# Third attention's lead in another order on three engines, and the wait for its last stores moved past a block boundary

## The chip, the core and the metric

The kernel runs on one core of one Trainium2 chip. The metric is the device time of one launch in microseconds (us), the median of several runs. The core has a matrix engine (PE), a vector engine (DVE), a scalar engine (ACT), a general-purpose engine (POOL) and a sequencer that only issues transfers here (SP). Each runs its own list of instructions in order; between them there are only semaphores.

## The reference

Two layers of a hybrid network over 1024 tokens of width 256, in float32. Layer 0 runs twice "attention, then a mixture of 64 experts" (block-causal attention, then windowed attention). Layer 1 runs "full attention, feed-forward, latent attention, feed-forward". What matters here is the first part of layer 1, the third attention of the kernel:

```python
Xn = (X - mu) * rsqrt(var + 1e-5) * ln_w + ln_b          # X is itself a layer norm of the stream
Q, K, V = split(Xn @ W_in)                                # 16 heads of 16, over 4 x 256 tokens
Q, K = rope(Q), rope(K)                                   # interleaved pairs, first 8 channels of a head
probs = softmax(Q @ K.T / sqrt(16))                       # nothing is masked
out = (probs @ V) @ W_out + X
```

In this launch x is (1, 1024, 256), so that each query sees all 1024 keys.

## The kernel before

The program is two blocks, one behind the other. Class First (its engines' lists are First.sync, .tensor, .scalar, .gpsimd and .vector) holds both layers of experts with the attentions before them (tags a and b), and then the **lead** of the third attention (tag c). Class Second begins with the third attention itself. Between the two stands Core.clear_semaphores: at the end of a block every engine waits for the others, then GpSimd clears First's semaphores, in ranges, and all engines meet once more. Semaphores made with keep=True are left out of the clearing; they keep their counts into Second. So nothing of Second starts before the slowest engine of First has come to its end.

**What the lead computes.** The projection Q, K of tile t (128 tokens) goes to PSUM (Projection.project, `project(t)`), ACT copies it out (`copy(t)`), and DVE (even tiles) or POOL (odd tiles) rotates it (`rotate`: two products into a side buffer, a product and a sum in place). For exact products in bfloat16 each value is then held as a sum of three bfloat16 parts. That is done in eight units n, each a chunk of 128 rows for one half of the tokens:

- `turn(n)` on PE: four transposes into PSUM bank 4 or 5. Waits for the rotations of its half, and for rest(n-2), which frees the bank.
- `part1(n)` on ACT: PSUM to the first part.
- `rest(n)` on DVE: PSUM minus the first part, into one of three buffers.
- `part2(n)` on ACT: rest to the second part.
- `part3(n)` on POOL for even n, on DVE for odd n: rest minus the second part.
- `store(n)` on SP: the three parts to DRAM, 384 KB. In Second, SP issues 78 transfers that read them back, stacked by head (Projection.stack).

The first stacks are not read back but made on the chip: `make(n)` on PE, n = 0 to 11, is three matmuls that pick rows out of the three parts of a unit (unit 0 for n = 0 to 3, unit 1 for 4 to 7, unit 4 for 8 to 11), into PSUM bank 6 or 7; `mcopy(n)` copies the result out, on ACT for even n and on DVE for odd n, and frees the bank for make(n+2).

**The order before.** PE: turn 0, 1, 2, 3 between and behind the last projections; make 0 to 3; turn 4; make 4 to 7; turn 5, 6, 7; make 8 to 11. ACT, DVE and POOL have their own lists written out by hand to match (First.scalar, First.vector, First.gpsimd). At the end of First.sync stands

```python
for n in range(1, 2 * c.per_half):
    c.store(sp, n)
sp.wait_ge(c.parts_stored, 16 * 2 * c.per_half)
```

and in Second.sync `c.stack(sp, h, g, 0)`, whose 0 says that no wait is wanted.

**Ahead of the lead.** The norm of the second half of the tokens is turned by PE into banks 6 and 7 (`norm.turn(pe, 4, 1, (6, 7))`, L289); ACT takes one bank to xT (L315) and DVE the other (`norm.store_vector(4, 1)`, L326). project(4) waits for both. On DVE `rotate(0)` and `rotate(2)` of tiles 0 and 2 stand before that store. The first attention has the same pattern with `norm.store_vector(0, 1)` (L329).

Lines: project L534, copy L545, rotate L584, L587 and L590, turn L609, part1 L615, rest L622, part2 L628, part3 L636, store L652, stack L670 and L674, make L744, mcopy L754, the clearing L98, the meeting of all engines L100.

Of the kernel before, what the change touches and what calls it, by code (L numbers as in the profile page):

```python
# [449 lines left out]
class Projection:  # L450
# [5 lines left out]
    def __init__(self, core, cfg, places, made, wo=None):  # L456
# [8 lines left out]
        if tag != "c":  # L465
# [3 lines left out]
            core.sem(f"{tag}_{n}") for n in ("ones", "p1", "r1", "p2", "pst"))  # L469
# [185 lines left out]
    def stack(self, sp, h, g, stored):  # L655


        cfg, kv = self.cfg, self.cfg.kv_heads
        if stored:
            sp.wait_ge(self.parts_stored, 16 * stored)  # L660
        c, r = g // 2, 64 * (g % 2)
        k0, k1 = (0, kv) if kv < HEADS else (QUART * g, QUART * g + QUART)
        if kv < HEADS and g:
            k0 = k1
        while k0 < k1 and ("k", k0, h) in self.made.stacks[self.tag]:
            k0 += 1
        for s, (pq, pk) in enumerate(PAIRS):
            rows = slice(s * HD, (s + 1) * HD)
            if ("q", QUART * g, h) not in self.made.stacks[self.tag]:
                sp.dma_start(self.qs[h][rows, 4 * g:4 * g + 4, :],  # L670
                             self.parts_dram[h, pq, c, r:r + 64, :].rearrange("(h d) t -> d h t", d=HD)).then_inc(self.stacked[h][g], 16)
            if k0 < k1:
                r0 = k0 % 8 * HD
                sp.dma_start(self.ks[rows, k0:k1, h * HALF:(h + 1) * HALF],  # L674
                             self.parts_dram[h, pk, QC + k0 // 8, r0:r0 + (k1 - k0) * HD, :].rearrange(
                                 "(h d) t -> d h t", d=HD)).then_inc(self.stacked[h][g], 16)
# [1548 lines left out]
class First:  # L2225
# [26 lines left out]
    def sync(self, sp):  # L2252
# [21 lines left out]
        c = self.c  # L2274
# [4 lines left out]
        sp.wait_ge(c.parts_stored, 16 * 2 * c.per_half)  # L2279
# [32 lines left out]
    def tensor(self, pe):  # L2312
# [68 lines left out]
        for t, n in ((4, None), (5, 0), (6, 1), (7, 2), (None, 3)):  # L2381
            if t is not None:
                c.project(pe, t)
            if n is not None:
                c.turn(pe, n)
        for n in range(4):
            self.made.make(pe, c, n)
        c.turn(pe, 4)
        for n in range(4, 8):
            self.made.make(pe, c, n)  # L2390
        for n in range(5, 8):
            c.turn(pe, n)
        for n in range(8, 12):
# [65 lines left out]
    def scalar(self, act):  # L2459
# [62 lines left out]
        c.copy(act, 7)  # L2522
        c.take_part1(act, 2)
        c.take_part2(act, 1)
        c.take_part1(act, 3)
        c.take_part2(act, 2)
        c.take_part2(act, 3)
        for n in (0, 2):
            self.made.copy(act, nc.scalar.copy, c, n)
        c.take_part1(act, 4)  # L2530
        c.take_part2(act, 4)
        for n in (4, 6):
            self.made.copy(act, nc.scalar.copy, c, n)
        c.take_parts(act, 5, 8)
        for n in (8, 10):
            self.made.copy(act, nc.scalar.copy, c, n)
# [115 lines left out]
    def vector(self, dve):  # L2652
        core, norm, start, moe = self.core, self.norm, self.start, self.moe
        nc = core.nc
        for h in range(2):
# [5 lines left out]
            for t in range(4 * h, 4 * h + 4):  # L2661
                norm.scale(dve, 0, t)
            norm.store_vector(dve, 0, h, 1, (4 + 2 * h, 5 + 2 * h))
        a, b, c = self.a, self.b, self.c
        for t in (0, 2):
            a.rotate(dve, nc.vector, 0, t)
# [36 lines left out]
        for t in (0, 2):  # L2703
            c.rotate(dve, nc.vector, 0, t)
        norm.store_vector(dve, 4, 1, 1, (6, 7))
        c.rotate(dve, nc.vector, 0, 4)
# [4 lines left out]
        c.take_rest(dve, 2)  # L2711
        c.take_rest(dve, 3)
        c.take_part3(dve, nc.vector, 3)
        for n in (1, 3):
            self.made.copy(dve, nc.vector.tensor_copy, c, n)
        c.take_rest(dve, 4)
        for n in (5, 7):
            self.made.copy(dve, nc.vector.tensor_copy, c, n)
        c.take_rest(dve, 5)
        c.take_part3(dve, nc.vector, 5)  # L2720
        c.take_rest(dve, 6)
        c.take_rest(dve, 7)
        for n in (9, 11):
            self.made.copy(dve, nc.vector.tensor_copy, c, n)
# [116 lines left out]
class Second:  # L2841
# [40 lines left out]
    def sync(self, sp):  # L2882
        core, c, attend, down, folded, latent = self.core, self.c, self.attend, self.down, self.folded, self.latent
        for g in range(4):
            for h in range(2):
                c.stack(sp, h, g, 0)
# [618 lines left out]
```

## Time and profile before

| | us |
|---|---|
| three runs | 1932.94, 1930.66, 1927.86 |
| median | 1930.66 |
| the profiled execution | 1929.17 |
| its span, first to last instruction | 1927.4 |

| engine | busy us | share of the span |
|---|---|---|
| PE | 1811.5 | 94% |
| DVE | 1077.3 | 56% |
| ACT | 912.8 | 47% |
| POOL | 694.9 | 36% |

The busy shares are means over many stages. The lead of the third attention takes the stretch from about 1203 to 1242 us of the span, 2% of it. All rows below are of the profiled execution. In a timeline a row is a run of equal instructions on one engine; behind it, in brackets, stands how long the engine had been idle before it and what ended that. "PEclk" is the clock that the chip granted TensorE, 1.00 for its upper level (2.4 GHz) and 0.50 for its lower (1.2 GHz).

### The profile page before, as it was taken

How to read it: one execution, taken by the hardware profiler on the slowest of the kernel's cores; microseconds unless marked ns; L12 is line 12 of the kernel's file. 1: busy time of each engine (PE TensorE's matmuls, PEld its weight loads, DVE VectorE, ACT ScalarE, POOL GpSimd, SP SyncE). 2: the span in 40 equal slices, each digit the busy share in tenths (PEclk: the TensorE clock that was granted, in tenths of full speed). 3: DMA queues.
4: the chain of work that ended last, by engine and by line, in shares of the span. 5: the costliest groups of instructions: out<-in, count | busy, mean ns of one | idle time of the engine just before them, and what ended most of it. 6: DMA issues, size and time to landing. Idle time of an engine off the chain costs nothing. (4 is left out here: it accounts for less than half of the span.)

```text
span 1927.4 us, 30327 instructions
## 1 busy us (share of the span) xinstructions
PE 1811.5 (94%) x10570; PEld 1244.4 (65%) x10580; DVE 1077.3 (56%) x1854; ACT 912.8 (47%) x1934; POOL 694.9 (36%) x627
## 2 busy tenths in 40 slices
PE   6899799999999898899999999699998999999998
PEld 3333688888887565688888886333334677777776
DVE  6875444444445564444444446588865666555544
ACT  3687433333333565333333333368874456445431
POOL 5200366666664110366666664400001344212200
PEclk8899999999999999999999999899999999999999
DMA  4300444444440310544444440290001000000000
GB/s 126 96 1 1 103 125 115 110 114 110 111 110 1 104 37 1 136 103 104 114 114 114 114 117 1 94 176 17 1 1 22 1 1 2 1 1 2 1 12 12
DMA packets 136969, 121.72 MB, mean 63 GB/s; under 512 B 84354, under 2 KB 122714, under 8 KB 136634
## 3 DMA queue, kind: packets, MB, share of 16 engines
q1 hardware_dynamic: 136857, 120.24, 25.3%
q8 instruction: 69, 1.13, 0.3%
q14 instruction: 43, 0.34, 0.1%
HBM read 111.41 MB, written 8.65 MB: 62 GB/s over the span
## 5 line engine op out<-in xcount | busy, mean ns | idle before, releaser
L1395 DVE TENSOR_TENSOR e_inner_lo<-e_inner,e_inner_hi 128x512 fp32r<-128x512 f32 x192 | 246.8, 1286 | 393.6 <-ACT e_inner_hi L1364 393.4
L1383 POOL TENSOR_TENSOR e_wsilu<-e_silu,e_rw 128x512 f32<-128x512 f32 x192 | 262.0, 1364 | 225.3 <-ACT e_silu L1358 166.2
L1334 PE MATMUL psum<-e_x_hi,e_w_hi 128*128 128x512 f32 x768 | 303.7, 395 | 6.7 <-DVE e_inner L1403 6.7
L1334 PE MATMUL psum<-e_x_lo,e_w_hi 128*128 128x512 f32 x768 | 299.6, 390 | 0.0
L1334 PE MATMUL psum<-e_x_hi,e_w_lo 128*128 128x512 f32 x768 | 299.4, 390 | 0.0
L1358 ACT ACTIVATE e_silu<-psum 128x512 f32<-128x512 f32 x192 | 114.8, 598 | 350.9 <-PE psum L1334 350.9
L1390 POOL TENSOR_TENSOR e_w_lo<-e_raw,e_w_hi 128x384 fp32r<-128x384 f32 x180 | 220.5, 1225 | 129.1 <-ACT e_w_hi L1371 115.9
L1334 PEld LDWEIGHTS psum<-e_x_hi,e_w_hi 128*128 128x128 f32 x768 | 144.4, 188 | 48.3 <-DVE e_inner L1403 16.9
L1090 DVE TENSOR_REDUCE c_mx<-psum 128x1 f32<-128x1024 f32 x128 | 150.5, 1219 | 28.2 <-PE psum L959 27.6
L1334 PEld LDWEIGHTS psum<-e_x_hi,e_w_lo 128*128 128x128 f32 x768 | 144.5, 188 | 30.7
L1334 PEld LDWEIGHTS psum<-e_x_lo,e_w_hi 128*128 128x128 f32 x768 | 144.5, 188 | 29.1
L1053 ACT ACTIVATE c_probs<-psum 128x512 f32<-128x512 f32 x256 | 136.4, 600 | 48.0 <-PE psum L991 45.4
L1349 PE MATMUL psum<-e_inner_hi,e_w_hi 128*128 128x512 f32 x384 | 151.1, 394 | 7.5 <-DVE e_inner_lo L1395 7.5
L1403 DVE TENSOR_TENSOR e_inner<-psum,e_wsilu 128x512 f32<-128x512 f32 x192 | 130.5, 680 | 43.4 <-POOL e_wsilu L1383 43.4
L1371 ACT CAST e_w_hi<-e_raw 128x384 fp32r<-128x384 f32 x180 | 92.4, 513 | 123.0 <-PE psum L1349 121.9
L1349 PE MATMUL psum<-e_inner_lo,e_w_hi 128*128 128x512 f32 x384 | 150.0, 391 | 0.0
L1349 PE MATMUL psum<-e_inner_hi,e_w_lo 128*128 128x512 f32 x384 | 149.9, 390 | 0.0
L2137 DVE TENSOR_REDUCE l_negmax<-psum 128x1 f32<-128x128 f32 (+7 forms) x128 | 96.7, 756 | 80.4 <-PE psum L1964 79.9
L1364 ACT CAST e_inner_hi<-e_inner 128x512 fp32r<-128x512 f32 x192 | 118.0, 614 | 31.3 <-DVE e_inner L1403 31.3
L2063 ACT COPY l_probsT<-psum 128x512 f32<-128x512 f32 (+2 forms) x96 | 46.1, 480 | 151.4 <-PE psum L1976 151.0
L2054 ACT ACTIVATE l_probs<-psum,l_negmax 128x128 f32<-128x128 f32 (+7 forms) x128 | 95.3, 744 | 18.4 <-DVE l_negmax L2137 16.3
L1090 DVE TENSOR_REDUCE a_mx<-psum 128x1 f32<-128x384 f32 (+7 forms) x128 | 91.2, 751 | 20.9 <-PE psum L959 20.1
(355 smaller groups left out, 3180.8 us busy)
## 6 DMA issues: line engine op xcount, KB each, us to landing
e_rw<-e_rw_dram SPq DMA_DIRECT2D x60, 384.0 KB, 5.3
e_rw<-e_rw_dram SPq DMA_DIRECT2D x60, 256.0 KB, 5.3
e_raw<-in_L_ffn_w_gate SPq DMA_DIRECT2D x64, 192.0 KB, 2.6
e_raw<-in_L_ffn_w_up SPq DMA_DIRECT2D x64, 192.0 KB, 2.6
e_raw<-in_L_ffn_w_down SPq DMA_DIRECT2D x32, 384.0 KB, 3.6
e_rw<-e_rw_dram SPq DMA_DIRECT2D x68, 128.0 KB, 4.9
c_parts_dram<-c_part SPq DMA_DIRECT2D x8, 384.0 KB, 2.5
a_qs<-a_parts_dram SPq DMA_DIRECT2D x42, 64.0 KB, 2.3
```

The source lines that it names most:

```text
L1053: nc.scalar.activation(self.probs[:, self.step_of[p, j] % 2, x, 0:nq], self.ring_bank(("scores", p, j, x))[:, 0:nq], ACT.Exp, scale=HD ** ...
L1090: nc.vector.tensor_reduce(self.mx[:, p % 2, t % QUART, x:x + 1], self.max_buffer(n)[:, 0:cfg.max_width(t)], AX_X, ALU.max).then_inc(self.m ...
L1334: last = nc.tensor.matmul(bank[u % 2][:], self.w[a][s][:, KC * which + k, j * P:(j + 1) * P], self.x[b][:, k, h * HALF:(h + 1) * HALF], st ...
L1349: last = nc.tensor.matmul(self.obank[2 * h + m][:], flat[:, j * D + m * P:j * D + (m + 1) * P], self.inner_parts[b][:, u % 3, :], start=fi ...
L1358: self.core.nc.scalar.activation(self.silu[:, u % 2, :], self.gbank[u % 2][:], ACT.Silu).then_inc(self.silu_done, 1)
L1364: self.core.nc.scalar.copy(self.inner_parts[0][:, u % 3, :], self.inner[:, u % 2, :]).then_inc(self.high_made, 1)
L1383: self.core.nc.gpsimd.tensor_tensor(self.wsilu[:, u % 2, :], self.silu[:, u % 2, :], self.rw[s][:, j, h * HALF:(h + 1) * HALF], ALU.mult). ...
L1390: self.core.nc.gpsimd.tensor_tensor(self.w[1][1 - s][:, p, :], self.raw[:, p, :], self.w[0][1 - s][:, p, :], ALU.subtract).then_inc(self.w ...
L1395: self.core.nc.vector.tensor_tensor(self.inner_parts[1][:, u % 3, :], self.inner[:, u % 2, :], self.inner_parts[0][:, u % 3, :], ALU.subtr ...
L1403: self.core.nc.vector.tensor_tensor(self.inner[:, u % 2, :], self.ubank[u % 2][:], self.wsilu[:, u % 2, :], ALU.mult).then_inc(self.inner_ ...
L2054: self.core.nc.scalar.activation(self.probs[t % 2][:, a, 0:w], self.scores_of(m, a)[:, 0:w], ACT.Exp, bias=self.negmax[:, n % 4:n % 4 + 1] ...
L2137: self.core.nc.vector.tensor_reduce(self.negmax[:, n % 4:n % 4 + 1], self.scores_of(m, a)[:, 0:(t + 1) * P], AX_X, ALU.max, negate=True).t ...
```

## The change

Four edits. The lists of PE, ACT and DVE in the lead of the third attention are put in another order, in which the turns, the parts and the makes alternate. The wait for the stores is taken from the end of First.sync, and each stack of Second waits for them instead; for that their semaphore is kept past the clearing. On DVE rotate(2) of the third attention now stands behind the store of the norm. In the first attention rotate(0) now stands before it. No instruction of an engine that computes is added or removed.

```diff
-            core.sem(f"{tag}_{n}") for n in ("ones", "p1", "r1", "p2", "pst"))
+            core.sem(f"{tag}_{n}", keep=(tag, n) == ("c", "pst")) for n in ("ones", "p1", "r1", "p2", "pst"))
...
     def stack(self, sp, h, g, stored):
-        if stored:
-            sp.wait_ge(self.parts_stored, 16 * stored)
+        sp.wait_ge(self.parts_stored, 16 * stored)
...
         for n in range(1, 2 * c.per_half):
             c.store(sp, n)
-        sp.wait_ge(c.parts_stored, 16 * 2 * c.per_half)
```

In First.tensor:

```diff
-        for t, n in ((4, None), (5, 0), (6, 1), (7, 2), (None, 3)):
-            if t is not None:
-                c.project(pe, t)
+        for t, n in ((4, None), (5, 0), (6, 1), (7, 2)):
+            c.project(pe, t)
             if n is not None:
                 c.turn(pe, n)
-        for n in range(4):
+        for n in range(2):
+            self.made.make(pe, c, n)
+        c.turn(pe, 3)
+        for n in range(2, 4):
             self.made.make(pe, c, n)
         c.turn(pe, 4)
-        for n in range(4, 8):
+        for n in range(4, 6):
             self.made.make(pe, c, n)
-        for n in range(5, 8):
-            c.turn(pe, n)
-        for n in range(8, 12):
+        c.turn(pe, 5)
+        for n in range(6, 8):
+            self.made.make(pe, c, n)
+        c.turn(pe, 6)
+        for n in range(8, 10):
+            self.made.make(pe, c, n)
+        c.turn(pe, 7)
+        for n in range(10, 12):
             self.made.make(pe, c, n)
```

In First.scalar:

```diff
         c.copy(act, 7)
+        c.take_part2(act, 1)
         c.take_part1(act, 2)
-        c.take_part2(act, 1)
+        self.made.copy(act, nc.scalar.copy, c, 0)
+        c.take_part2(act, 2)
         c.take_part1(act, 3)
-        c.take_part2(act, 2)
+        self.made.copy(act, nc.scalar.copy, c, 2)
+        c.take_part1(act, 4)
         c.take_part2(act, 3)
-        for n in (0, 2):
-            self.made.copy(act, nc.scalar.copy, c, n)
-        c.take_part1(act, 4)
         c.take_part2(act, 4)
-        for n in (4, 6):
-            self.made.copy(act, nc.scalar.copy, c, n)
-        c.take_parts(act, 5, 8)
-        for n in (8, 10):
-            self.made.copy(act, nc.scalar.copy, c, n)
+        self.made.copy(act, nc.scalar.copy, c, 4)
+        c.take_part1(act, 5)
+        self.made.copy(act, nc.scalar.copy, c, 6)
+        c.take_part2(act, 5)
+        c.take_part1(act, 6)
+        self.made.copy(act, nc.scalar.copy, c, 8)
+        c.take_part2(act, 6)
+        c.take_part1(act, 7)
+        self.made.copy(act, nc.scalar.copy, c, 10)
+        c.take_part2(act, 7)
```

In First.vector, first attention:

```diff
             for t in range(4 * h, 4 * h + 4):
                 norm.scale(dve, 0, t)
+            if h:
+                self.a.rotate(dve, nc.vector, 0, 0)
             norm.store_vector(dve, 0, h, 1, (4 + 2 * h, 5 + 2 * h))
         a, b, c = self.a, self.b, self.c
-        for t in (0, 2):
-            a.rotate(dve, nc.vector, 0, t)
+        a.rotate(dve, nc.vector, 0, 2)
```

In First.vector, third attention:

```diff
-        for t in (0, 2):
-            c.rotate(dve, nc.vector, 0, t)
+        c.rotate(dve, nc.vector, 0, 0)
         norm.store_vector(dve, 4, 1, 1, (6, 7))
+        c.rotate(dve, nc.vector, 0, 2)
         c.rotate(dve, nc.vector, 0, 4)
         c.take_rest(dve, 0)
         c.take_rest(dve, 1)
         c.rotate(dve, nc.vector, 0, 6)
         c.take_part3(dve, nc.vector, 1)
         c.take_rest(dve, 2)
+        self.made.copy(dve, nc.vector.tensor_copy, c, 1)
         c.take_rest(dve, 3)
+        self.made.copy(dve, nc.vector.tensor_copy, c, 3)
+        c.take_rest(dve, 4)
         c.take_part3(dve, nc.vector, 3)
-        for n in (1, 3):
-            self.made.copy(dve, nc.vector.tensor_copy, c, n)
-        c.take_rest(dve, 4)
-        for n in (5, 7):
-            self.made.copy(dve, nc.vector.tensor_copy, c, n)
+        self.made.copy(dve, nc.vector.tensor_copy, c, 5)
         c.take_rest(dve, 5)
+        self.made.copy(dve, nc.vector.tensor_copy, c, 7)
+        c.take_rest(dve, 6)
         c.take_part3(dve, nc.vector, 5)
-        c.take_rest(dve, 6)
+        self.made.copy(dve, nc.vector.tensor_copy, c, 9)
         c.take_rest(dve, 7)
-        for n in (9, 11):
-            self.made.copy(dve, nc.vector.tensor_copy, c, n)
+        self.made.copy(dve, nc.vector.tensor_copy, c, 11)
         c.take_part3(dve, nc.vector, 7)
```

In Second.sync:

```diff
-                c.stack(sp, h, g, 0)
+                c.stack(sp, h, g, 2 * c.per_half)
```

## Rows read from the trace of the kernel before

**Rows 1.** Timeline of PE: start us, us, engine, line, operation [idle before].
```profile
1203.00 1.04 PE L289 MATMUL psum<-ident,xi 128*128 128x128 f32 x8
1206.99 3.67 PE L534 MATMUL psum<-c_w,xT 128*128 128x512 f32 x8 [2.95 <-issue]
...
1215.83 1.47 PE L744 MATMUL psum<-c_part,m_pick_q 128*96 128x512 bf16 x6
1220.94 2.79 PE L744 MATMUL psum<-c_part,m_pick_q 128*96 128x512 bf16 x6 [3.64 <-ACT c_qs L754]
...
1242.50 1.91 PE L959 MATMUL psum<-c_ks,c_qs 96*128 96x512 bf16 x4 [6.73 <-PEq L100]
...
1263.26 2.08 PE L959 MATMUL psum<-c_ks,c_qs 96*128 96x512 bf16 x4 [0.28 <-DVE c_mx L1090]
```

**Rows 2.** Timeline of SP, start and length of an issue, around the block boundary.
```profile
1237.18 0.36 SPq L652 DMA_DIRECT2D c_parts_dram<-c_part  x1
...
1241.93 3.16 SPq L670 DMA_DIRECT2D c_qs<-c_parts_dram  x7
```

**Rows 3.** The stores (L652) as the view of their line shows them.
```profile
DMA to landing us min/median/max: 2.5/2.5/4.7
```

**Rows 4.** The clearing between the blocks (L98), durations in ns min/median/max.
```profile
L98 POOLq DRAIN  x4: 73/98/136, 1240.1 to 1241.3; - x4
L98 POOLq EVENT_SEMAPHORE_RANGE_CLEAR  x4: 110/221/355, 1240.3 to 1241.4; - x4
```

**Rows 5.** Timeline of DVE in the lead.
```profile
1206.09 0.80 DVE L326 TENSOR_SCALAR xT<-psum,col_L_attn_a_ln_w,col_L_attn_a_ln_b 128x512 f32<-128x512 f32 x1
...
1214.57 1.47 DVE L584 TENSOR_TENSOR c_moved<-c_qk,c_sin 128x128 f32<-128x128 f32 x2
...
1217.26 1.20 DVE L636 TENSOR_TENSOR c_part<-c_rest,c_part 128x512 bf16<-128x512 f32 x1
1218.38 1.27 DVE L622 TENSOR_TENSOR c_rest<-psum,c_part 128x512 f32<-128x512 f32 x2
...
1221.41 0.68 DVE L754 CAST c_qs<-psum 96x512 bf16<-96x512 f32 x1
...
1236.41 0.68 DVE L636 TENSOR_TENSOR c_part<-c_rest,c_part 128x512 bf16<-128x512 f32 x1
```

**Rows 6.** Timeline of ACT in the lead.
```profile
1204.08 0.78 ACT L315 ACTIVATE xT<-psum,col_L_attn_a_ln_b,col_L_attn_a_ln_w 128x512 f32<-128x512 f32 x1 [0.29 <-PE psum L289]
...
1215.49 0.59 ACT L615 CAST c_part<-psum 128x512 bf16<-128x512 f32 x1
...
1219.10 1.22 ACT L628 CAST c_part<-c_rest 128x512 bf16<-128x512 f32 x2 [2.01 <-DVE c_rest L622]
1220.22 0.57 ACT L754 CAST c_qs<-psum 96x512 bf16<-96x512 f32 x1
```

**Rows 7.** Timeline of POOL in the lead.
```profile
1214.52 1.16 POOL L636 TENSOR_TENSOR c_part<-c_rest,c_part 128x512 bf16<-128x512 f32 x1 [0.51 <-ACT c_part L628]
...
1217.99 1.04 POOL L590 TENSOR_TENSOR c_qk<-c_qk,c_moved 128x256 f32<-128x256 f32 x1
```

**Rows 8.** Timeline of DVE in the lead of the first attention.
```profile
13.35 1.38 DVE L274 TENSOR_SCALAR xn<-x,n_mv,n_inv 128x256 f32<-128x256 f32 x4
19.25 0.69 DVE L329 COPY xT<-psum 128x512 f32<-128x512 f32 x1 [4.51 <-PE psum L289]
...
24.44 0.69 DVE L590 TENSOR_TENSOR a_qk<-a_qk,a_moved 128x320 f32<-128x320 f32 x1
```

**Rows 9.** Timeline of PE in the lead of the first attention.
```profile
25.27 1.04 PE L609 MATMUL psum<-ident,a_qk 128*128 128x128 f32 x8
```

**Rows 10.** Stretches A:B: length, busy us per engine (instructions), PEclk, DMA share.
```profile
35.30:55.60 20.30, 14.98 (x57) 6.60 (x58) 15.13 (x36) 9.05 (x15) 7.81 (x15) 0.50 0.54 135
...
1219.70:1226.40 6.70, 5.46 (x15) 2.96 (x16) 3.13 (x4) 2.71 (x6) 1.15 (x1) 0.50 0.53 173
...
1240.20:1246.90 6.70, 4.40 (x11) 2.67 (x13) 2.35 (x2) 1.86 (x3) 4.84 (x5) 0.50 0.30 88
```

## Prediction, made before the changed kernel ran

> **What bounds the kernel now.** The page comes first: PE is busy 94% of the span, DVE 56%, ACT 47%. That says little of the stretch that is changed, so the second view is the timeline of PE around it. There PE is not the bound: it stands still for 2.95 us before project(4), for 3.64 us before make(2), and for 6.73 us before the first matmul of the second block, which is released by the meeting of all engines [rows 1]. What counts is therefore when the slowest engine ends the first block, and behind it the boundary itself. The timelines of SP and DVE give that end: DVE's last part3 starts at 1236.41 and takes 0.68 us, SP issues store(7) at 1237.18, and SP's next transfer, the first of the second block, is at 1241.93 [rows 5, 2]. The third view is the clearing between the blocks [rows 4], the fourth the granted clock by stretches [rows 10]. Because the boundary is a barrier for all five engines, each us by which the first block ends earlier is a us off the total, unless the clock of the second block gives it back.
>
> **Part 1, the rotation of tile 2 moved behind the norm's store.** The turned norm is ready for ACT at 1204.08; DVE takes its bank only at 1206.09, behind rotate(2), for 0.80 us, and project(4) starts at 1206.99, 0.10 us after that store ends [rows 6, 5, 1]. Now DVE is free at 1203.8, when rotate(0) ends, and stores at 1204.08 as ACT does: to 1204.88, so project(4) starts at 1204.98. That is 2.01 us earlier, and copy(4) to copy(7), turns 0 to 2 and what hangs on them follow by 2.01. Is rotate(2) late then? It would start at 1204.8 and, at the 2.3 us that lay between the ends of rotate(0) and rotate(2), end at 1207.1; turn(0) wants it at 1208.5 and DVE itself rotate(4) at 1207.7. So it hides, with 0.6 us to spare. **Gain 2.0.**
>
> **Part 2, the same kind of move in the first attention.** rotate(0) goes into a gap of DVE: its scaling ends at 14.73 and the store waits for PE until 19.25 [rows 8]. Both rotations together took 5.2 us behind that store (19.94 to 25.13), one some 2.6, so the store isn't delayed. But nobody waited for it: the last rotation that turn(0) needs ended at 25.13, and PE went into turn(0) at 25.27 straight from the projections, without idle time [rows 8, 9]. **Gain 0**, bounds 0 and 0.1; a loss would need a rotation longer than 4.5 us.
>
> **Part 3, the lead in another order.** I walk the new lists by hand with these durations. A make holds PE for 0.65 us and its result is there after 0.81 (six matmuls of two makes: 1.47); with the clock at its lower level two makes take 2.79 [rows 1]. A turn, four of the eight transposes in 1.04 us, holds PE for 0.44 and is done after 0.60 [rows 1]. part1 is 0.59, part2 0.62, mcopy 0.57 on ACT and 0.68 on DVE; rest is 0.68 [rows 5, 6]. Two instructions in a row on one engine overlap by 0.02 to 0.1 us, as two part2 in 1.22 and two rests in 1.27 show [rows 5, 6]. part3 is 1.16 on POOL [rows 7]; on DVE it took 1.20 beside POOL's rotation and 0.68 at the end, when POOL was idle [rows 5, 7]. A hand-over takes 0.03 to 0.04 us to ACT and DVE and 0.14 to PE. Walked in this way with the old lists, and PE at the lower level from 1219.65 to 1226.5, the lead ends at 1237.06; the trace has 1237.09 [rows 5].
>
> The new chain, with part 1 already in: DVE's rotate(6) starts at 1212.56 (was 1214.57 [rows 5]) and ends at 1215.33; part3(1), beside POOL's rotate(7), to 1216.43; rest(2) 1216.37 to 1217.06; mcopy(1) to 1217.66; PE make(3) at 1217.80, turn(4) at 1218.45, done 1219.05; ACT part1(4) to 1219.68; DVE rest(4) to 1220.40; ACT part2(4) to 1221.05, mcopy(4) to 1221.53; PE make(6) 1221.68, make(7) 1222.32, turn(6) 1222.97 to 1223.57; part1(6) to 1224.20; rest(6) to 1224.92; part3(5) to 1225.51; mcopy(9) to 1226.11; make(11) 1226.26 to 1227.07; mcopy(11) to 1227.79; part3(7) ends at 1228.39. From the start of rotate(6) that is 15.83 us where it was 22.53 (1214.57 to 1237.09). **Gain 6.7.** In the old order turns 5 to 7 stood behind makes 4 to 7, and makes 8 to 11 behind the turns; the new one fills those waits. Moved waits: mcopy(0) on ACT now stands ahead of part2(2) and waits for make(0), 0.1 us; behind it nothing is late. On SP the stores are 1.1 us apart or more and each issue is 0.36 [rows 2], so their queue stays hidden.
>
> **Part 4, the wait for the last stores.** Store(7) is issued in 0.36 us and lands 2.5 us after its start [rows 2, 3]: at 1239.68. SP is the last engine, so 2.5 - 0.36 = 2.14 us of waiting go. What is late next is SP's own issue, 0.45 us behind DVE. The kept semaphore lies between others that are cleared, so it cuts a range in two, and GpSimd does one drain and one clear more. Four pairs lie between 1240.1 and 1241.6; the cheapest pair is 73 + 110 ns, the dearest 136 + 355 [rows 4]. A split adds no semaphore, so I take the cheap end, 0.2. **Gain 1.9.** The wait comes back in front of the stacks: store(7) issued at 1228.48 lands at 1230.98, and SP enters the second block at 1231.3, so it waits for nothing. Even at the longest landing seen, 4.7 [rows 3], the stacks would be 1.9 us late. The first six of them, the queries of phase 1, are issued within 3.16 us [rows 2] of 1241.93, and PE asks for them at 1263.26 [rows 1]: hidden, by over 15 us. Of an outstanding transfer at a block's end the trace shows nothing: between 0 and the whole 2.14 could stay. I take 0, because no row shows an engine held there by anything but its own work.
>
> **The clock.** The sum so far is 2.0 + 6.7 + 2.1 - 0.2 = 10.6. It assumes the upper level in the lead. The opening of the second block ran at the lower level from its start at 1242.5 to about 1246.9, behind 6.73 us of idle PE [rows 1, 10]. Now PE idles 4.8 us (1227.1 to 1231.9), still long, and the two lower stretches here last 6.7 us [rows 10]; if one begins just behind PE's start, it covers 6.7 us of work where it covered 4.4. At half speed 2.3 us more cost 1.1 at most; bounds: -2.2 (no lower stretch in the opening) and +1.1. I take +1.1, since the idle time is nearer to the old 6.73 than to none. **Net gain 9.5.**
>
> The profiled execution took 1929.17 us for a span of 1927.4, so it would become 1919.7. It lies 1.5 below the median of the runs; on the median the forecast is 1930.66 - 9.5 = 1921.1.
>
> **The rivals.** (B) *The clock falls inside the lead.* It did so from 1219.7 on, behind the 3.64 us gap [rows 1, 10]. The new order leaves a shorter gap there, 1.6 us before make(3), but the rows don't say how short is short enough. With the lower level over the same 6.8 us the walk ends at 1230.45, 2.1 later: gain 7.4, 1923.2. The Trainium skill (TensorE: Matmul & The Clock Gate, Terms) puts the penalty at the throttled time times one half; by that the price would be 3.4 and the time 1924.6. (C) *VectorE and GpSimd hold each other up.* part3 on DVE took 1.20 beside POOL against 0.68 [rows 5, 7]. In the walk DVE's part3(5) ends 0.14 us before POOL's part3(6) begins; if both late ones on the chain collide, 2 x 0.5 = 1.0 us go: 1922.1. The Trainium skill (GPSIMD Engine Reference, 1. Specifications) has the SBUF interfaces shared where a DVE instruction has two SBUF inputs, as part3 has; the row agrees, the rest of the lead reads PSUM. (D) *The block's end waits for the outstanding transfer*: 2.14 stay, 1923.2. (E) *The new lists stall on each other*, so that part 3 brings nothing: 2.0 + 1.9 = 3.9, less 1.1: 1927.9. Against it speaks that the same walk gives the old end to 0.03 us. (F) *Slower.* A long stretch at the lower level behind the boundary. At the kernel's start it lasted over 20 us, from 35.3 to 55.6 [rows 10]. Behind phase 0's maxima the third attention keeps PE busy, so each us there costs half a us: 21 us more than before cancel the 10.6, 33 make the kernel 0.3% slower, 1936.5. No later stretch in this trace was that long.
>
> **How the numbers follow.** Forecast with its clock term 0.56; B 0.16; C 0.08; D 0.07; opening at the upper level, near 1918, 0.05; E 0.05; F 0.03. A measurement of this kernel can tell about 0.3% from no change, 5.8 us, so faster means under 1924.9: the forecast, B to D and the good opening, less 0.08 for combinations such as B with D (1925.3): 0.84. Same: E and those, 0.12. Slower: F, 0.04. The three runs before spread by 5 us, so a median can lie 1.5 off. The range goes from 1917.5 (all of the 10.6, and a median 2.5 low) to 1926.0 (B with D, and a little).
>
> **What would show it.** In the profile after: project(4) at 1204.98 with under 1 us of idle before it; part3(7) on DVE ending near 1228.4; store(7) at 1228.5; five drain-and-clear pairs in place of four; SP's first stack about 2.8 us after store(7), and PE's first matmul of the second block near 1231.9. From there on all stages keep their lengths. A gap of over 2 us before make(2) or make(3), the lower level inside the lead, or SP's first stack more than 3.5 us after store(7) would show a step wrong.

## Result and profile after

| | before | after |
|---|---|---|
| median us, six runs each | 1927.58 | 1913.85 |
| lowest and highest | 1924.24, 1932.94 | 1911.48, 1918.35 |
| the profiled execution | 1929.17 | 1913.68 |
| its span | 1927.4 | 1911.9 |

The changed kernel is faster: the ratio of the two is 0.9932, with an interval from 0.9918 to 0.9946, or 13.1 us by the ratio (13.7 between the medians). The forecast was 1921.1 with a range from 1917.5 to 1926.0. The direction was right, but the time lies 3.6 us below the range. (Before's median of six includes the three runs of the table ahead of the prediction, whose own median is 1930.66.)

The page of the kernel after: its span, the busy times, and the granted clock in 40 slices.

```profile
span 1911.9 us, 30329 instructions
...
PE 1807.4 (95%) x10570; PEld 1243.0 (65%) x10580; DVE 1074.9 (56%) x1854; ACT 911.8 (48%) x1934; POOL 694.4 (36%) x627
...
PEclk9899999999999999999999999999999999999999
```

The busy times moved by some 4 us at most, and every engine has as many instructions as before. What changed is where the engines stand still, so the timelines have to be read. PE in the lead and at the start of the second block (answers to [rows 1]):

```profile
1199.48 1.04 PE L289 MATMUL psum<-ident,xi 128*128 128x128 f32 x8
1201.47 3.67 PE L534 MATMUL psum<-c_w,xT 128*128 128x512 f32 x8 [0.95 <-ACT xT L315]
...
1214.29 0.82 PE L742 MATMUL psum<-c_part,m_pick_q 128*96 128x512 bf16 x3 [1.44 <-ACT c_part L628]
...
1228.25 1.92 PE L957 MATMUL psum<-c_ks,c_qs 96*128 96x512 bf16 x4 [4.67 <-PEq L100]
```

DVE, where the norm's store and the last part3 stand ([rows 5]), then the POOL instruction between them ([rows 7]), then SP around the boundary ([rows 2]), and last the clearing ([rows 4]):

```profile
1200.56 0.81 DVE L326 TENSOR_SCALAR xT<-psum,col_L_attn_a_ln_w,col_L_attn_a_ln_b 128x512 f32<-128x512 f32 x1 [0.27 <-PE psum L289]
...
1221.33 0.68 DVE L636 TENSOR_TENSOR c_part<-c_rest,c_part 128x512 bf16<-128x512 f32 x1
...
1224.22 0.68 DVE L636 TENSOR_TENSOR c_part<-c_rest,c_part 128x512 bf16<-128x512 f32 x1
```

```profile
1222.15 1.16 POOL L636 TENSOR_TENSOR c_part<-c_rest,c_part 128x512 bf16<-128x512 f32 x1 [3.37 <-ACT c_part L628]
```

```profile
1224.98 0.36 SPq L652 DMA_DIRECT2D c_parts_dram<-c_part  x1
1227.75 3.15 SPq L668 DMA_DIRECT2D c_qs<-c_parts_dram  x7
```

```profile
L98 POOLq DRAIN  x5: 57/90/136, 1225.7 to 1227.1; - x5
L98 POOLq EVENT_SEMAPHORE_RANGE_CLEAR  x5: 45/178/356, 1225.9 to 1227.2; - x5
```

To compare two executions, each is measured from one event ahead of all edits of this stretch, the turning of the norm on PE (L289): 1203.00 before [rows 1], 1199.48 after. The second mark is SP's first transfer of the second block, 1241.93 before [rows 2], 1227.75 after. The 15.5 us of span then divide so:

| stretch | before | after | difference |
|---|---|---|---|
| start to the norm's turn | 1203.00 | 1199.48 | -3.52 |
| turn to SP's first transfer (lead and boundary) | 38.93 | 28.27 | -10.66 |
| from there to the end | 685.45 | 684.14 | -1.3 |

The middle row was forecast at 10.6. So the edits did what the steps say, to 0.1 us, and what is to be explained is the 3.5 us ahead of them and the 1.3 behind, where 1.1 had been expected the other way.

The granted clock of the kernel after in stretches (length, busy us of PE, PEld, DVE, ACT, POOL with instructions, PEclk, DMA share, GB/s; answers to [rows 10]):

```profile
30.80:34.20 3.40, 3.40 (x10) 1.52 (x9) 2.61 (x3) 1.20 (x2) 3.24 (x5) 0.50 0.60 171
44.50:54.70 10.20, 8.21 (x34) 3.22 (x34) 7.41 (x18) 5.16 (x9) 5.14 (x13) 0.50 0.54 125
1212.00:1225.40 13.40, 9.07 (x48) 5.12 (x46) 10.53 (x16) 8.76 (x16) 4.91 (x5) 1.00 0.58 189
1225.60:1232.20 6.60, 3.95 (x10) 2.35 (x12) 2.36 (x2) 1.78 (x3) 4.39 (x4) 0.50 0.43 135
```

The lead runs wholly at the upper level; the lower one comes while PE idles at the boundary and covers 4.0 us of the second block (1228.25 to about 1232.3). One more follows some 14 us later, as in the kernel before, where [rows 10] don't show it (after, then before):

```profile
1246.00:1252.40 6.40, 5.62 (x23) 1.95 (x24) 6.26 (x10) 0.95 (x2) 0.00 (x0) 0.50 1.20 124
```

```profile
1260.70:1267.20 6.50, 5.98 (x25) 2.08 (x26) 6.36 (x10) 1.31 (x3) 0.00 (x0) 0.50 1.20 124
```

At the kernel's start two lower stretches of 13.6 us together stand in place of before's 20.3.

### The profile page after: what moved, and what is told of

It is laid out like the page before. It is cut to its first block and busy times, and to the rows that moved or that the text cites. A ratio compares the mean times of both kernels' runs of the same rounds, so it can differ in the third digit from the quotient of the medians.

```text
span 1911.9 us, 30329 instructions
## 1 busy us (share of the span) xinstructions
PE 1807.4 (95%) x10570; PEld 1243.0 (65%) x10580; DVE 1074.9 (56%) x1854; ACT 911.8 (48%) x1934; POOL 694.4 (36%) x627
```

## Experiments

Two theories went into them. A: the four edits do what the walk says and add up, and the surplus is the clock and a transfer elsewhere, which the edits don't touch. B: the surplus belongs to the change, either because an edit is worth more than the walk gives it (the first attention's rotation, which lies ahead of the 3.5 us, or the order, by keeping PE supplied), or because the edits help each other. Each of the four parts was run alone, then the whole change again on two chips, then kernels in which PE's idle time is filled.

In the tables "lead and boundary" is the stretch from the norm's turn to SP's first transfer, 38.93 before and 28.27 after. In the texts of the expectations the stretch of 39.5 us ends instead at PE's first matmul of the second block, some 0.6 us later.

**Part 2 alone.** Only the rotation of the first attention is moved.

```diff
                 norm.scale(dve, 0, t)
+            if h:
+                self.a.rotate(dve, nc.vector, 0, 0)
             norm.store_vector(dve, 0, h, 1, (4 + 2 * h, 5 + 2 * h))
...
-        for t in (0, 2):
-            a.rotate(dve, nc.vector, 0, t)
+        a.rotate(dve, nc.vector, 0, 2)
```

> Only the first attention's rotation(0) is moved ahead of the norm's store. Theory A (the changed kernel's 3 us ahead of the third attention's lead are clock and transfer luck): nothing waited for this rotation, time 0 +- 1.5 us against before, and the stretch from the lead's norm turn to the second block's first matmul stays at 39.5 us. Rival B (the edit itself brings them, by freeing VectorE in the first attention's lead): 2 to 3.5 us faster in the median, and the first attention's first shift starts a microsecond or more earlier whatever the clock does.

Median 1927.09 (11 runs) against 1926.65 (29 runs of the kernel before, shared with the next three), ratio 1.0000 with 0.9991 to 1.0009. DVE in the first attention's lead, and PE's turn:

```profile
14.58 0.55 DVE L584 TENSOR_TENSOR a_moved<-a_qk,a_sin 128x160 f32<-128x160 f32 x2
...
15.69 0.49 DVE L590 TENSOR_TENSOR a_qk<-a_qk,a_moved 128x320 f32<-128x320 f32 x1
20.47 0.69 DVE L329 COPY xT<-psum 128x512 f32<-128x512 f32 x1 [4.29 <-PE psum L289]
```

```profile
26.50 1.04 PE L609 MATMUL psum<-ident,a_qk 128*128 128x128 f32 x8
```

The rotation is done in DVE's gap, and PE goes into turn(0) without idle time, as before [rows 9]. That turn(0) starts 1.2 us later than in before's profile is not the edit's: in the executions with part 1 or part 3 alone, whose code is the old one here, it starts at 26.51 and 26.56. Nobody waited for the rotation: nothing is gained, and theory B's first form falls. Its profiled execution also shows what the clock can do to the lead. A lower stretch of 6.6 us fell on the projections, which no edit of this kernel touches, and they took 6.73 us in place of 3.67:

```profile
1205.80 6.73 PE L534 MATMUL psum<-c_w,xT 128*128 128x512 f32 x8 [2.95 <-issue]
```

Lead and boundary were 41.62 there, 2.7 more than before, where the expectation had them unchanged.

**Part 1 alone.** The rotation of tile 2 goes behind the norm's store.

```diff
-        for t in (0, 2):
-            c.rotate(dve, nc.vector, 0, t)
+        c.rotate(dve, nc.vector, 0, 0)
         norm.store_vector(dve, 4, 1, 1, (6, 7))
+        c.rotate(dve, nc.vector, 0, 2)
```

> Only the third attention's rotation(2) is moved behind the norm's store. Theory A: project(4) starts 2.0 us earlier behind its turn, the stretch from the turn (L289) to the second block's first matmul goes from 39.5 to 37.5 us; total 2 us less. Rival B (the lead has slack that swallows it): the stretch stays above 38.5.

Median 1923.84 (11 runs), ratio 0.9984 with 0.9975 to 0.9993. Two rows of PE and two of SP:

```profile
1198.83 1.04 PE L289 MATMUL psum<-ident,xi 128*128 128x128 f32 x8
1200.82 3.67 PE L534 MATMUL psum<-c_w,xT 128*128 128x512 f32 x8 [0.95 <-ACT xT L315]
```

```profile
1231.01 0.36 SPq L652 DMA_DIRECT2D c_parts_dram<-c_part  x1
1235.76 2.22 SPq L670 DMA_DIRECT2D c_qs<-c_parts_dram  x5
```

The idle time before project(4) falls from 2.95 to 0.95 us, and lead and boundary are 1235.76 - 1198.83 = 36.93: 2.00 less, all of it arriving at the boundary. By the medians it is 2.8. The granted clock falls inside the lead here too, and make(2) to turn(4) take as long as before.

**Part 3 alone.** The new lists of PE, ACT and DVE, with the rotation and the wait for the stores as before (the edit is the three list diffs that stand ahead of the prediction; on PE it begins so):

```diff
-        for n in range(4):
+        for n in range(2):
+            self.made.make(pe, c, n)
+        c.turn(pe, 3)
+        for n in range(2, 4):
             self.made.make(pe, c, n)
```

> Only the new order of turns, parts and makes on TensorE, ScalarE and VectorE. Theory A: the stretch goes from 39.5 to 32.8 us (6.7 less), total 6.7 less, plus or minus what the clock does in the second block's opening. Rival B (the order alone doesn't work without the earlier start): less than 5 us of the stretch.

Median 1918.15 (5 runs), ratio 0.9962 with 0.9949 to 0.9975.

```profile
1199.71 1.04 PE L289 MATMUL psum<-ident,xi 128*128 128x128 f32 x8
```

```profile
1227.21 0.36 SPq L652 DMA_DIRECT2D c_parts_dram<-c_part  x1
1231.95 2.26 SPq L669 DMA_DIRECT2D c_qs<-c_parts_dram  x5
```

From turn to first transfer 32.24 us, 6.69 less than before; the walk had 6.7. The boundary itself is as before, 4.74 us from store(7) to the first stack. The median moved by 8.5, 1.8 more than the stretch. That the 1.8 are clock elsewhere is likely but not shown: its five runs have 0.984 to 0.987, the runs of before 0.978 to 0.986.

**Part 4 alone.** The semaphore is kept, the wait goes to the stacks.

```diff
-        sp.wait_ge(c.parts_stored, 16 * 2 * c.per_half)
...
-                c.stack(sp, h, g, 0)
+                c.stack(sp, h, g, 2 * c.per_half)
```

> Only the wait for the last stores is moved into the second block. Theory A: 2.14 us of waiting go and 0.2 us of clearing come, the stretch goes from 39.5 to 37.6 us; store(7)'s issue to the second block's first transfer goes from 4.75 to 2.8 us. Rival B (the block's end waits for the transfer in flight): 4.75 us stay, plus the fifth clearing.

Median 1925.83 (12 runs), ratio 0.9989 with 0.9974 to 1.0003: by the medians alone nothing to be told from no change. SP shows it:

```profile
1234.37 0.36 SPq L652 DMA_DIRECT2D c_parts_dram<-c_part  x1
1237.13 3.20 SPq L670 DMA_DIRECT2D c_qs<-c_parts_dram  x7
```

From store(7) to the first stack are 2.76 us where 4.75 were [rows 2]: 1.99 less, with five drain-and-clear pairs. The store lands 2.5 us after its start at the earliest [rows 3], so it is still in flight while the clearing goes on, and no engine waits for it. The three stretches of parts 1, 3 and 4 add up to 2.00 + 6.69 + 1.99 = 10.68, against 10.66 for the whole change. Theory B's form in which the edits help each other falls here.

This execution also had 23.6 us at the lower level near the start, in code that is the same as before's:

```profile
35.80:59.40 23.60, 18.60 (x68) 7.49 (x72) 17.60 (x39) 11.54 (x20) 7.82 (x15) 0.50 0.55 134
```

**The whole change again, on two chips.** No edit; each with runs of the kernel before beside it.

> The changed kernel as it is, on the chip of the other three, as their measure. Theory A (10.7 us by the rows of the lead and the boundary, and 2 to 4 us by less time at TensorE's lower level): 12 to 14 us less than before, with a granted clock 0.003 above its. Rival B (only the 10.7 us): 10 to 11 us less at the clock of before.

> The changed kernel once more, beside the one with five. Theory A (what it brought above 10.7 us on the first chip was the clock's luck): 10 to 12.5 us below before. Rival B (a lasting gain beyond the lead and the boundary): 13 us or more below before.

| | median after | before beside it | ratio (interval) | lead and boundary |
|---|---|---|---|---|
| first comparison | 1913.85 | 1927.58 | 0.9932 (0.9918 to 0.9946) | 28.27 |
| second, its own chip | 1915.90 | 1927.25 | 0.9938 (0.9925 to 0.9950) | 28.27 |
| third, another chip | 1916.50 | 1925.89 | 0.9950 (0.9938 to 0.9963) | 28.27 |

The lead and the boundary repeat to 0.01 us. The gain by medians is 13.7, 11.4 and 9.4, a mean of 11.5. The first repetition lies between the two forecasts made for it (12 to 14, and 10 to 11). The second lies just below theory A's 10 to 12.5 and far from rival B's 13 or more. So comparisons of the same two kernels differ by 4 us while the edited stretch doesn't. The two repetitions also settle the 1.3 us behind the boundary: from SP's first transfer to the end they take 685.6 us each, where before has 685.45. Nothing is gained there.

**The order before, with PE kept busy.** Part 3 may gain for two reasons: the stages stand better, or PE, with shorter gaps, keeps its upper level. To part them, 14 matmuls on zeros, whose result nobody uses, fill PE's wait ahead of make(2) in the old order.

```diff
-        for n in range(4):
+        for n in range(2):
+            self.made.make(pe, c, n)
+        pe.wait_ge(c.copied, 5)
+        keep_warm(core, 14)
+        for n in range(2, 4):
             self.made.make(pe, c, n)
...
+def keep_warm(core, n):
+    for _ in range(n):
+        core.nc.tensor.matmul(core.bank[0][:], core.ident_h[:], core.zero_h[:], start=True, stop=True)
```

> The kernel before, with 14 idle-filling matmuls on zeros (512 columns, 3.0 us, result unused) between make(1) and make(2), where TensorE stood still for 3.64 us. Nothing else waits for them. Theory A (part of what the new order brought is the clock, which falls in the lead behind that gap): the lead stays at the upper level, the stretch from the norm's turn to SP's first transfer of the second block goes from 38.93 to 37.4 us, and the median is 1.5 to 3 us below before. Rival B (the clock falls for another reason, or its price is hidden): stretch and time unchanged within 0.5 us.

Median 1927.21, ratio 0.9997 with 0.9988 to 1.0006. Rows of PE, and the clock over the whole lead:

```profile
1201.92 1.04 PE L289 MATMUL psum<-ident,xi 128*128 128x128 f32 x8
...
1216.05 3.19 PE L2227 MATMUL psum<-zero_h,ident_h 128*128 128x512 bf16 x14
1219.86 0.82 PE L744 MATMUL psum<-c_part,m_pick_q 128*96 128x512 bf16 x3 [0.63 <-ACT c_qs L754]
```

```profile
1205.00:1237.00 32.00, 22.42 (x98) 11.80 (x98) 17.44 (x28) 14.43 (x26) 10.85 (x13) 1.00 0.31 101
```

The lower stretch that before had in the lead [rows 10] is gone, and lead and boundary are 37.85 us, 1.08 less, where theory A had 37.4. That is what those 6.7 us at the lower level had cost there. So of part 3's 6.7 us, 5.6 are the order and 1.1 the clock that comes with it. The median doesn't show the 1.1, where theory A had 1.5 to 3: lower stretches came elsewhere instead, or it is lost in the spread. The runs don't tell which.

**The boundary, with PE kept busy.** On the changed kernel, seven such matmuls behind make(11) and eight between the blocks fill all but about 1.2 of PE's 4.67 us of idle time.

```diff
         for n in range(10, 12):
             self.made.make(pe, c, n)
+        pe.wait_ge(c.copied, 8)
+        keep_warm(core, 7)
...
         first.build()
+        keep_warm(core, 8)
         core.clear_semaphores()
```

> The changed kernel, with 7 such matmuls behind make(11) and 8 between the blocks, so that TensorE's idle time of 4.7 us over the boundary shrinks to about 1 us. Theory A (the lower level in the second block's opening comes from that idle time and costs half of its 4 us): the opening runs at the upper level, 1.5 to 2.5 us less than the changed kernel. Rival B (VectorE's maxima bound the opening anyway, or the clock falls one stretch later): same time within 1 us. If the matmuls delay the boundary, SP's first transfer comes later than 2.76 us behind store(7).

Median 1914.10, ratio 0.9928 with 0.9915 to 0.9941. The changed kernel beside it had 1915.90 with 0.9925 to 0.9950, so the two are not told apart by the medians.

```profile
1226.15 1.89 PE L2225 MATMUL psum<-zero_h,ident_h 128*128 128x512 bf16 x8 [0.71 <-PEq L2836]
1228.48 0.38 PE L1020 MATMUL psum<-zero_h 128*128 128x512 bf16 x1 [0.45 <-PEq L100]
1228.70 1.03 PE L957 MATMUL psum<-c_ks,c_qs 96*128 96x512 bf16 x4
```

```profile
1226.00:1232.00 6.00, 5.38 (x24) 2.93 (x25) 2.67 (x3) 1.86 (x3) 3.58 (x3) 1.00 0.36 113
...
1244.00:1253.80 9.80, 9.21 (x32) 2.90 (x32) 8.74 (x11) 2.90 (x6) 0.00 (x0) 0.50 1.20 125
```

The opening now runs at the upper level (four matmuls in 1.03 us, 1.92 in the changed kernel). The opening is measured from SP's first transfer to the rest of DVE's first shift (c_mrest, L1102; L1104 in the kernel before). It takes 20.43 us; it was 22.58 before, 22.30 after, and 22.64 and 22.60 in the two repetitions. So the lower level there costs about 2.1, and theory A's 1.5 to 2.5 is met in this stretch. But a lower stretch follows at 1244, 10.2 us long. The changed kernel has one near there too, from 1245.9 on for 6.8 us, so 3.4 us of the 4.0 that were removed came back there, as rival B had it. Eight matmuls are also too many: they end behind the clearing, SP starts 3.02 us behind store(7) in place of 2.76, and lead and boundary are 28.52.

**The same, and the last part3 ahead of the last copy.** In addition DVE does part3(7) before mcopy(11), and the semaphores of part3 are kept as well, so that the cleared ranges are four again.

```diff
         c.take_rest(dve, 7)
-        self.made.copy(dve, nc.vector.tensor_copy, c, 11)
         c.take_part3(dve, nc.vector, 7)
+        self.made.copy(dve, nc.vector.tensor_copy, c, 11)
...
-        self.part3 = [core.sem(f"{tag}_p3{e}") for e in range(2 if tag == "c" else 1)]
+        self.part3 = [core.sem(f"{tag}_p3{e}", keep=tag == "c") for e in range(2 if tag == "c" else 1)]
```

> As the kernel with the warm boundary, and two trims: part3(7) stands ahead of mcopy(11) on VectorE, so that store(7) is issued 0.5 us earlier, and the semaphores of part3 are kept too, so that four ranges are cleared and not five (0.2 us). Theory A: 0.6 us less of the stretch from the norm's turn to SP's first transfer than the changed kernel's 28.26; the median alone can't show that. Rival B (mcopy(11), now last on VectorE, ends the block): 0.2 us less.

Median 1914.06, ratio 0.9930 with 0.9918 to 0.9942: as without it.

```profile
1224.68 0.69 DVE L636 TENSOR_TENSOR c_part<-c_rest,c_part 128x512 bf16<-128x512 f32 x1 [0.68 <-ACT c_part L628]
```

part3(7) now waits 0.68 us for ACT's part2(7): store(7) comes only 0.25 us sooner, since part2(7) is the next latest. Lead and boundary are 1228.51 - 1200.21 = 28.30: 0.22 less than in the kernel without these two edits (28.52), but no less than in the changed kernel (28.27), where theory A had 0.6 less and rival B 0.2. So nearly all of the 0.25 arrives. The clear that is saved doesn't, because the eight matmuls still end behind the clearing (3.05 us from store(7) to the first stack). What was taken away on DVE stood a quarter of a us ahead of the next thing.

**Five matmuls between the blocks.** The changed kernel with seven matmuls behind make(11), five between the blocks, and part3's semaphores kept; mcopy(11) stays ahead of part3(7).

```diff
+        keep_warm(core, 5)
         core.clear_semaphores()
```

> The changed kernel with 7 filling matmuls behind make(11), 5 between the blocks instead of 8, and the semaphores of part3 kept as well, so that four ranges are cleared. In the warm boundary with 8, two of them ended behind the clearing and held the meeting up by 0.26 us. Theory A: from store(7) to SP's first transfer 2.6 us (2.76 less 0.17 of clearing), the opening at the upper level with its first shift at 20.4 us behind SP's first transfer (22.3 to 22.6 in the changed kernel), total 1 to 2.5 us below the changed kernel. Rival B: the clock falls one stretch later and takes it back, total within 1 us of the changed kernel.

Median 1911.88, ratio 0.9933 with 0.9918 to 0.9949. The changed kernel on the same chip (the third comparison) had 1916.50, so it is 4.6 us better by the medians, more than the 1 to 2.5 that were expected. The two intervals overlap (0.9938 to 0.9949), so that the whole kernel is better is not shown by the medians. It has the lowest median of the versions run.

```profile
1224.30 0.36 SPq L652 DMA_DIRECT2D c_parts_dram<-c_part  x1
1226.91 3.20 SPq L668 DMA_DIRECT2D c_qs<-c_parts_dram  x6
```

```profile
1225.11 1.24 PE L2225 MATMUL psum<-zero_h,ident_h 128*128 128x512 bf16 x5 [0.71 <-PEq L2836]
...
1227.23 1.03 PE L957 MATMUL psum<-c_ks,c_qs 96*128 96x512 bf16 x4
```

```profile
1226.00:1232.00 6.00, 5.31 (x25) 3.22 (x24) 4.13 (x4) 2.27 (x5) 5.04 (x5) 1.00 0.37 110
...
1242.80:1249.20 6.40, 5.72 (x22) 1.68 (x20) 6.26 (x10) 0.57 (x2) 0.00 (x0) 0.50 1.19 119
```

From store(7) to the first stack are 2.61 us, 0.15 less than in the changed kernel, and the opening takes 20.33. Here the store's landing stands level with the end of the clearing: it lands 2.5 us after its start, at 1226.8, and SP's wait for it is at 1226.8. So more taken off the boundary would meet the landing next. From the norm's turn to the end of the opening that is 28.12 + 20.33 = 48.45 us, where the changed kernel on this chip has 28.27 + 22.60 = 50.87: 2.4 us of the 4.6 are in the stretch that the edit touches. The rest is not shown to be its work. The lower stretch behind the boundary (last row) is as long as in the changed kernel.

## Why the prediction's four gains were right, and its clock term and its anchor wrong

**Part 1, right.** project(4) was forecast at 1204.98 in the times of before; less the 3.52 us that the whole stretch came sooner that is 1201.46, and the row has 1201.47, with 0.95 us of idle time. Alone the edit is worth 2.00. rotate(2) stayed hidden.

**Part 2, right.** No gain (the ratio lies between 0.9991 and 1.0009), and PE goes into turn(0) without idle time.

**Part 3, right.** The walk ended part3(7) at 1228.39; less the 3.52 that is 1224.87, and the rows give 1224.22 + 0.68 = 1224.90. The wait before make(3) was forecast at 1.6 us and is 1.44. Alone the order is worth 6.69. The walk assumed the upper level through the lead, and that held.

**Part 4, right.** Forecast 1.9, measured 1.99 alone. The forecast had 2.14 of waiting removed and 0.2 for the fifth pair. In the trace 2.19 go, the clearing takes 0.13 us longer from its first drain to its last clear than with four, and SP's own wait instruction ahead of the first stack, which the forecast had at nothing, takes some 0.07. That the two small errors cancel is luck. Nobody waits for the landing of store(7): it lands 2.5 us after its start, at 1227.5, and SP's wait for it comes at 1227.7. The forecast had a margin of 0.3 us there, and it is 0.2.

**The clock, wrong.** This is the step that failed: the term "I take +1.1". It took the opening of the second block to lose 1.1 us more than before, because a lower stretch of 6.7 us that begins behind PE's start would cover more work. But the row that it cites has the stretch begin at 1240.20 [rows 10], 2.3 us ahead of PE's start at 1242.50 [rows 1]. It began ahead again, while PE idled, and covered 4.0 us of work in the first profiled execution and 4.6 to 4.7 in the repetitions, where before had 4.4. The opening changed by -0.28, +0.06 and +0.02 us in the three profiled executions of the changed kernel: the right size of the term is 0. Its lower bound, -2.2, was sized well: where PE is kept busy the opening is 2.1 shorter.

**What no step had: the rest of the kernel.** 3.52 us of the profiled difference lie ahead of the lead. About 1.5 are there by 83 us, where after has 13.6 us at the lower level and before 20.3. About 1.6 come between 206 and 237, where SP waits for the landing of the experts' rows (how long it waited in total, how often, and the longest; before, then after):

```profile
SPq L1237 <- DMA e_rw_dram<-e_rwT: 5.2, 2, 3.4
```

```profile
SPq L1235 <- DMA e_rw_dram<-e_rwT: 3.6, 2, 1.8
```

Neither follows from the edits. The kernels with part 1, 3 or 4 alone run the same instructions as before up to the norm's turn, and they reach it at 1198.83, 1199.71 and 1200.19; the old order with PE kept busy reaches it at 1201.92. So identical code spreads over 4.2 us here, and before's 1203.00 is the latest of all executions. The three with one part also wait 3.6 us in all for the rows; part 1 and part 3 show the short pattern of the clock near the start, while part 4 shows 23.6 us in one piece. The third comparison's execution has 4.5 us of the wait again. The 1.3 us behind didn't come back in either repetition. The sum over the profiled execution: forecast 9.5, plus 3.5 ahead, 1.1 for the failed term, and 1.3 behind, makes 15.4, and 15.5 were measured. Of the 1.3 behind, 0.28 is the opening's.

**The anchor, wrong too.** The forecast was set on 1930.66, the median of three runs; six gave 1927.58, and the larger samples 1926.65, 1927.25 and 1925.89. With the same gain of 9.5 and the median of six the forecast would have been 1918.1. "A median can lie 1.5 off" was too small: it lay 3 to 5 off. Of the 7.25 us between 1921.1 and 1913.85, 3.1 are the anchor and 1.1 the clock term. With both put right the forecast would have been 1917.0, already below the range. The last 3.1 are the surplus of the first comparison over the 10.66 of the trace. In the second it is 0.7 and in the third -1.3, so the first comparison was lucky, and no part of the change is shown to have earned it.

**How much of the time is the clock.** In 29 runs of the kernel before, those with a granted clock of 0.986 took 1924.1 to 1924.3 us, and the one with 0.978 took 1937.7. The difference of 0.008 is 0.008 x 2 x 1930 = 31 us more at the lower level, for 13.5 us of time: some 0.44 us for each. That rests on the two ends, one of them a single run. A straight line through all 29 gives 0.35, and one through the 17 or the 11 runs of the other two samples 0.26. The Trainium skill (TensorE: Matmul & The Clock Gate, Terms) has half of the throttled time. The runs give less over a whole kernel, and far less in the lead, 1.08 us for 6.7, because PE is not the bound there. In the opening, where about 4 us are removed for 2.1, they give the half.

**The rivals.** B, the clock inside the lead, didn't come: PEclk is 1.00 from 1212.0 to 1225.4, and the repetitions have the same 28.27. The lower stretch had cost the old order 1.08 us, about half of the rival's 2.1. C, VectorE and GpSimd against each other: DVE's part3(5) ends at 1222.01 and POOL begins at 1222.15, the 0.14 us of the walk, and the late part3 take 0.68 each. The Trainium skill (GPSIMD Engine Reference, 1. Specifications) on the shared interface was not put to the test by them. But the prediction's "the rest of the lead reads PSUM" is a misreading: the rotations have both inputs in SBUF. DVE's rotate(4), while POOL is idle, takes 1.41 us in the kernel after. Its rotate(6), the first step of the walked chain, takes 2.76 beside POOL's part3(0) and rotate(7), as it did before; their first products are in the rows below. The walk used that measured length, so its sum is right; the 1.3 us by which this rotation is longer are in both kernels. What it would take there without POOL was not tried. D, the outstanding transfer, fell with 2.76 us from store(7) to the first stack. E fell with 6.69. F didn't come: the next lower stretch behind the boundary is 6.8 us long.

```profile
1204.15 0.49 DVE L584 TENSOR_TENSOR c_moved<-c_qk,c_sin 128x128 f32<-128x128 f32 x2 [0.65 <-ACT c_qk L545]
...
1209.05 1.45 DVE L584 TENSOR_TENSOR c_moved<-c_qk,c_sin 128x128 f32<-128x128 f32 x2
```

**Open.** Whether the change lowers the time at the lower level elsewhere, by shifting when things happen, is not settled: the profiled executions have 0.987 against 0.982, but the repetitions 0.983 and up, and before's runs reach 0.986. It was not tried apart from the medians above.

## What to carry to other kernels

Measure an edit by the stretch between two events in the trace that enclose it, and the median only as the second witness: the stretch repeated to 0.01 us over three comparisons, while medians of the same pair of kernels gave gains of 9.4 to 13.7. A lead in which three engines hand work to each other can be walked from rows of the same trace; here the new order was worth what the walk said, 6.69 for 6.7. Take the anchor from more than three runs where the gain is about as large as their spread (5 us here). At a barrier, find all that ends within a few tenths of a us (here ACT's part2, PE's unused matmuls, the clearing, the landing of the store) before removing one: the next one takes its place.

## What the runs showed of the chip that was not expected

The end of this block doesn't wait for the transfer in flight (2.76 us from store(7) to the first stack, against 4.75 with the explicit wait). SP's drain takes 128 ns with store(7) outstanding, against 7 ns with nothing outstanding (after, then before). In the first case it also stands straight behind the issue, so which of the two makes it longer is not shown.

```profile
L2829 SPq DRAIN  x1: 128/128/128, 1225.4 to 1225.4; - x1
```

```profile
L2819 SPq DRAIN  x1: 7/7/7, 1239.9 to 1239.9; - x1
```

A fifth cleared range costs 0.13 us, less than the cheapest pair of four (73 + 110 ns), since the range that is split becomes two shorter ones: the shortest clear is 45 ns where it was 110.

The granted clock differs from run to run in identical code: from 30 to 60 us of the span, the profiled executions had 13.6, 20.3, 20.0 (3.2 and 16.8) and 23.6 us at the lower level. Keeping PE busy with unused matmuls removes the lower level from the place where they stand, and at the boundary it cost nothing where they ended ahead of the clearing. What it does to the later stretches varies: with eight the one that follows grew from 6.8 to 10.2 us, with five it stayed at 6.8 and came 2.5 us sooner (15.7 us behind SP's first transfer for 18.2).
